# A gated eight-layer network on one core: third attention and third feed-forward on pairs of batches, fourth attention three steps behind, and 128-row bias products

## Chip, core and metric

One core of a Trainium2 chip runs the whole program in one launch. The metric is the time of an execution on the device in microseconds, median of several executions. TensorE's clock has two levels, 1.2 and 2.4 GHz; the profile gives the granted clock as a share of the higher one.

## What is computed

The input x is 8 batches of 128 tokens with 128 features, the context the same shape. Four cross-attentions and four feed-forward layers alternate, each added to x with a gate:

```
x = x + tanh(g_xattn[i]) * attention_i(layernorm(x), ctx, ctx, mask)
x = x + tanh(g_ffn[i])   * ffn_i(layernorm(x))
```

Attention 0 has 16 heads of 64, attentions 1 and 3 have 16 heads of 8 with projections and output bias. Attention 2, which is called the third here, has one head of 128, uses the context itself as keys and values, and then a 128x128 output product with bias: `softmax(Q K^T / sqrt(D)) V @ W.T + b`. Feed-forward 0 and 3 are quantized products 128 to 512 to 128; 1 is a mixture of 8 experts, two per token; 2, called the third, is `layernorm(gelu(x @ fc.T)) @ proj.T` with ternary weights.

## The kernel before

All data stay in on-chip memory. Every engine runs an instruction stream of its own, in order; semaphores join them. The layers are numbered `A0, F0, A1, ROUTE, MOE, A2, F2, A3, F3`. A plan says which layers run in a step: layer L with offset `at` works in steps `at` to `at + 8 + LAG[L]`, one new batch per step. Inside a step each layer has four slots per engine; an entry `(lag, function)` runs the function for the batch that entered `lag` steps ago. `walk` takes the slots of all layers of a step in turn, one instruction from each, and so writes the order of each engine's stream. The third stretch of the program, after the experts, is

```
LAG = [3, 2, 3, 1, 2, 3, 2, 3, 2]
... + steps_of({A2: 0, F2: 4, A3: 8, F3: 12}))
```

So the third attention (A2) starts in step 0, the third feed-forward (F2) in step 4, the fourth attention (A3) in step 8, the fourth feed-forward (F3) in step 12, and there are 22 steps. A2's chain (normalize `xn`, transpose, `scores2` with the mask product, `shift2` for the maximum, `exps2`, `probsT2`, `pv2`, `norm2`, `ot`, `y`, `resid`) is spread over lags 0 to 3. F2's (`up`, `gelu2`, `hid2_stats`, `rs_hid`, `hid2_ln`, `ht`, `y_ffn`) over lags 0 to 2. A3's scores are four products of 4 heads (`scores`, groups 0 to 3) against `kz`, the keys spread over heads by GpSimd (`mask_keys`, two products of 128x1024 per batch). `inverse_root` on GpSimd gives 1/sqrt of each variance. GpSimd fetches the experts' rows for batch b two steps ahead (`fetch`). Biases come in through a product of a 1-row tile of ones with a 1-row tile (`row["bo_n"]`, `crow`), placed before the output product.

## Time and profile before

| | us |
|---|---|
| median of 3 executions | 603.82 (601.82 to 604.89) |
| the profiled execution, its own time | 603.31 |
| its span from first to last instruction | 601.5 |
| mean granted TensorE clock | 0.854 |

The span is read as three stretches: the first plan (attention 0 to routing) up to about 335 us, the experts up to about 380 us, then the third stretch, which the change rewrites. Line numbers in the rows are those of the kernel before: L838 is the bias product and L840 the output product of an attention, L868 up, L879 the transposes of the hidden layer, L887 and L890 bias and down product, L759 scores of A1 and A3, L850 scores of A2, L473 kz.

### The profile page before, as it was taken

What the parts mean: (1) busy time and instruction counts of PE and PEld (TensorE: products, weight loads), DVE (VectorE), ACT (ScalarE), POOL (GpSimd) and SP (SyncE); (2) the same over time, 40 slices, a digit from 0 to 9 for tenths busy, and PEclk for the clock granted to TensorE, in tenths of its full rate; (3) what the DMA queues carried; (4) which work ended last, traced back from release to release, by engine and by line L of the source; (5) the groups of instructions that cost most, each with busy time, mean ns of one, the idle gap of its engine ahead of it and who ended that gap; (6) DMA issues with size and microseconds to landing.
All of it is one profiled execution on the core that took longest, in us unless ns stands there. A gap on an engine that the chain in (4) does not pass through costs nothing.

```text
span 601.5 us, 8470 instructions
## 1 busy us (share of the span) xinstructions
PE 487.6 (81%) x2862; PEld 381.3 (63%) x2862; DVE 373.2 (62%) x1000; ACT 267.8 (45%) x525; POOL 187.7 (31%) x274
## 2 busy tenths in 40 slices
PE   5789899999976897788896499358879988888843
PEld 3577888778865675566685399335646766656721
DVE  1177787788778667667764211355468786886573
ACT  3355455455442444233341243035556665565452
POOL 6080000000213321344514200374244345453141
PEclk9999999999988978788895599855779998996755
DMA  8930000000000200000000231110000000000000
GB/s 357 391 132 2 1 0 2 2 0 1 2 1 0 107 2 0 1 9 6 13 10 18 92 103 60 36 35 19 1 0 1 2 1 0 2 0 1 2 0 35
DMA packets 7131, 21.74 MB, mean 36 GB/s; under 512 B 1217, under 2 KB 3505, under 8 KB 6706
## 3 DMA queue, kind: packets, MB, share of 16 engines
q1 hardware_dynamic: 6065, 19.11, 8.8%
q0 software_dynamic: 1024, 2.10, 1.2%
q8 instruction: 24, 0.39, 0.3%
q14 instruction: 18, 0.14, 0.1%
HBM read 14.33 MB, written 6.88 MB: 35 GB/s over the span
## 4 chain that ended last, share of the span: by engine, by line
PE 56%; DVE 19%; issue 9%; ACT 7%; POOL 5%; DMA 3%; SPq 0%; DVEq 0%; POOLq 0%; ACTq 0%
PE bank L759 7%; PE bank L784 6%; PE bank L767 5%; PE bank L754 4%; PE bank L801 4%; PE bank L924 3%; PE bank L780 3%; DVE xn L1095 3%; PE bank L915 3%; POOL rstd L442 3%; PE bank L796 3%; DVE prob L1126 2%; PE bank L747 2%; PE bank L890 2%; PE bank L735 2%
## 5 line engine op out<-in xcount | busy, mean ns | idle before, releaser
L440 POOL TENSOR_SCALAR rstd<-mv 128x1 f32<-128x1 f32 x64 | 13.2, 206 | 292.7 <-DVE mv L1080 290.2
L1120 DVE TENSOR_REDUCE mx<-bank 128x4 f32<-128x512 f32 x96 | 66.0, 688 | 61.2 <-PE bank L759 43.3
L527 ACT ACTIVATE prob<-prob 128x512 f32<-128x512 f32 x96 | 60.1, 626 | 60.9 <-DVE prob L1126 60.5
L519 ACT ACTIVATE probT<-bank 128x512 f32<-128x512 f32 (+1 forms) x104 | 59.0, 568 | 50.2 <-PE bank L767 48.8
L759 PE MATMUL bank<-kz,qT 128*128 128x512 f32 x128 | 76.6, 685 | 0.0
L767 PEld LDWEIGHTS bank<-pack,prob 128*128 128x128 f32 x384 | 52.1, 154 | 38.1 <-issue 27.8
L784 PEld LDWEIGHTS bank<-va,probT 128*128 128x128 f32 x512 | 71.8, 216 | 0.8 <-ACT probT L519 0.7
L784 PE MATMUL bank<-va,probT 128*128 128x9 f32 x512 | 69.9, 264 | 0.4 <-ACT probT L519 0.4
L1126 DVE TENSOR_TENSOR prob<-bank,mx 128x512 f32<-128x512 f32 x96 | 65.2, 679 | 2.5 <-PE bank L767 1.5
L767 PE MATMUL bank<-pack,prob 128*128 128x128 f32 x384 | 64.1, 294 | 1.3 <-ACT hid L617 1.3
L473 POOL TENSOR_TENSOR kz<-kT,pack 128x1024 f32<-128x1024 f32 x32 | 60.4, 1897 | 0.0
L1095 DVE TENSOR_SCALAR xn<-pack,mv,rstd 128x128 f32<-128x128 f32 x56 | 42.5, 773 | 17.7 <-POOL rstd L442 17.4
L519 ACT ACTIVATE xnT<-bank 128x128 f32<-128x128 f32 x48 | 13.2, 276 | 79.3 <-PE bank L735 75.3
L442 POOL TENSOR_TENSOR rstd<-rstd,minus_half 128x1 f32<-128x1 f32 x72 | 40.3, 560 | 6.0
L754 PE MATMUL bank<-kz,qT 128*128 128x256 f32 x128 | 33.3, 383 | 0.0
L780 PE MATMUL bank<-va,probT 128*128 128x65 f32 x256 | 32.8, 272 | 0.0
L780 PEld LDWEIGHTS bank<-va,probT 128*128 128x128 f32 x256 | 31.9, 196 | 0.0
L489 POOL DMA_INDIRECT moe_rows<-yrows_d,row_of x16 | 15.8, 985 | 51.7 <-DMA yrows_d<-o_n 47.9
L1103 DVE SCALAR_TENSOR_TENSOR pack<-bank,tanh_g,pack 128x128 f32<-128x128 f32 x40 | 13.8, 346 | 26.6 <-PE bank L840 14.6
L735 PE MATMUL bank<-pack,xn 128*128 128x128 f32 x40 | 14.3, 358 | 19.5 <-DVE xn L1095 14.9
L879 PE MATMUL bank<-pack,hid 128*128 128x128 f32 x96 | 19.8, 344 | 11.3 <-DVE hs L1244 5.1
L759 PEld LDWEIGHTS bank<-kz,qT 128*128 128x128 f32 x128 | 25.5, 218 | 4.8 <-issue 2.5
(212 smaller groups left out, 956.2 us busy)
## 6 DMA issues: line engine op xcount, KB each, us to landing
yrows_d<-moe_rows SPq DMA_DIRECT2D x2, 1510.0 KB, 19.8
pack<-pack_d SPq DMA_DIRECT2D x1, 2112.0 KB, 14.7
expert<-experts_d SPq DMA_DIRECT2D x4, 514.0 KB, 8.8
pack<-experts_d SPq DMA_DIRECT2D x4, 514.0 KB, 4.3
pack<-pack_d SPq DMA_DIRECT2D x1, 2048.0 KB, 9.6
xrows_d<-moe_rows SPq DMA_DIRECT2D x1, 1080.0 KB, 18.3
moe_rows<-xrows_d SPq DMA_DIRECT2D x8, 135.0 KB, 3.1
yrows_d<-o_n SPq DMA_DIRECT2D x8, 135.0 KB, 1.8
```

The source lines that it names most:

```text
L442: pool.tensor_tensor(out, out, minus_half, ALU.pow).then_inc(ev.sem, 1)
L473: pool.tensor_tensor(kz[:, it.k, 1024 * half:1024 * half + 1024].rearrange("p (h t) -> p h t", h=heads), kT[:, bass.ds(it.b, 1), :].to_bro ...
L519: act.activation(dst, src, ACT.Identity if kw else ACT.Copy, **kw).then_inc(E[layer][name].sem, 1)
L527: act.activation(prob[:, g % 2, :], prob[:, g % 2, :], ACT.Exp, scale=float(DK0 if layer == A0 else DK) ** -0.5).then_inc(E[layer]["probs" ...
L754: mm_ = pe.matmul(out[:, 256 * c:256 * c + 256], qT[:, it.k, P * t:P * t + P], kz[:, it.k, 256 * t:256 * t + 256], start=False, stop=(c == 1))
L759: mm_ = pe.matmul(out[:, :], qT[:, it.k, 0:P], kz[:, it.k, 512 * g:512 * g + 512], start=neg is None, stop=True)
L767: mm_ = pe.transpose(bank[T_BANK[g % 2]][:, P * j:P * j + P], prob[:, g % 2, P * j:P * j + P], ident)
L780: mm_ = pe.matmul(bank[O_BANK[g % 2]][:, VW0 * j:VW0 * j + VW0], probT[:, g % 2, P * j:P * j + P], va0[:, it.k, h, :], start=True, stop=True)
L784: mm_ = pe.matmul(bank[O_BANK[it.k]][:, VW * h:VW * h + VW], probT[:, g % 2, P * j:P * j + P], va[:, bass.ds(it.b, 1), h, :], start=True, ...
L1095: yield from do(dve.tensor_scalar(out, xs(it), mv[z][:, k, 0:1], rstd[z][:, k, 0:1], ALU.subtract, ALU.mult), hold=layer in (F0, F3))
L1120: yield from do(dve.tensor_reduce(m, src, AX.X, ALU.max))
L1126: yield from do(dve.tensor_tensor(prob[:, g % 2, :].rearrange("p (h t) -> p h t", h=GH), src, m.rearrange("p (h a) -> p h a", a=1).to_broa ...
```

## The change

- A2 and F2 work on two batches at a time (`PAIRS = 4` repetitions). Tiles get twice the width; each product, transpose, exp, gelu and normalization is still issued per batch, while evacuations of 128 columns, the maximum, the reciprocal, the division, the residual and the square root take both batches in one instruction.
- A2's lag is 1: scores, maximum, exp and transpose of a pair happen in the step in which it is normalized; PV to residual in the next.
- The offsets are A2 0, F2 1, A3 3, F3 7, which makes 17 steps.
- The softmax denominator comes from a column of ones behind the context, by PV, instead of from the exp's accumulator.
- All output biases of attentions 1 to 3 and `crow` are 128-row tiles with one row filled, multiplied by the 128x128 ones. `bv_3` stays one row.
- In routing, VectorE does the statistics ahead of the choice of experts.

```
-LAG = [3, 2, 3, 1, 2, 3, 2, 3, 2]
+PAIRS = B // 2
+REPS = [B, B, B, B, NE, PAIRS, PAIRS, B, B]
+LAG = [3, 2, 3, 1, 2, 1, 2, 3, 2]
...
-        + steps_of({A2: 0, F2: 4, A3: 8, F3: 12}))
+        + steps_of({A2: 0, F2: 1, A3: 3, F3: 7}))
...
 (GpSimd)
-                A2: [[(0, rs, A2)], [(0, fetch_ahead)], [], []],
-                F2: [[(0, rs, F2)], [], [(1, rs_hid)], []],
+                A2: [[(0, rs_2), (0, fetch_ahead)], [], [], []],
+                F2: [[], [], [(1, rs_hid)], [(0, rs_f)]],
 (ScalarE)
-                A2: [[(1, xt_sb, A2), (2, exps2)], [], [(3, ot_sb, A2), (2, probsT_sb2)], []],
-                F2: [[], [(1, gelu2), (2, hT_sb2)], [], [(0, xt_sb, F2)]],
+                A2: [[], [(1, ot_sb2), (0, xt_sb2)], [None, (0, exps2)], [(0, probsT_sb2)]],
+                F2: [[(2, hT_sbf, 1), (1, xt_sbf)], [(1, gelu_f, 0)], [(1, gelu_f, 1)], [(1, hT_sbf, 0)]],
 (TensorE)
-                pe.matmul(out, ones[0:1, :], row[f"bo_{n}"], start=True, stop=False)
+                pe.matmul(out, ones, col[f"bo_{n}"], start=True, stop=False)
...
+            def yf(it):
+                claim(it, F2, "y")
+                out = bank[R_BANK[1]][:, 0:W2]
+                pe.matmul(out.rearrange("p (a n) -> p a n", a=2), ones, both(crow[:, :]), start=True, stop=False)
+                for i in range(2):
+                    wait(pe, F2, "ht_sb", it, 1 + i)
+                    for t in range(FT):
+                        mm_ = pe.matmul(out[:, P * i:P * i + P], hT_f[it.k][:, F * i + P * t:F * i + P * t + P],
+                                        projw[:, P * t:P * t + P], start=False, stop=(i == 1 and t == FT - 1))
...
-                A2: [[(1, xt, A2)], [(3, ot, A2), (2, probsT2)], [(1, scores2)], [(2, pv2), (3, y, A2)]],
-                F2: [[(1, up, F2, "up", tern["fcT"][:, :], xnT[1])], [(2, ht, F2)], [None, None, (2, y_ffn, F2, projw)], [(0, xt, F2)]],
+                A2: [[(1, pv2)], [(1, ot2), (0, xt2)], [(1, y2), (0, scores2)], [(0, probsT2)]],
+                F2: [[(2, htf, 1), (2, yf), (1, xtf)], [(1, upf, 0)], [(1, upf, 1)], [(1, htf, 0)]],
 (VectorE)
-                A2: [[[(3, norm2), (0, sum_stats)]], [(0, ln, A2)], [], [(1, shift2), (3, resid, A2)]],
-                F2: [[(0, ln_stats, F2)], [(0, ln, F2)], [[(1, hid2_stats), (2, resid, F2)]], [(1, hid2_ln)]],
+                A2: [[[(1, norm2), (0, sum_stats)]], [(0, pair_ln, A2, xn_2, mv_2, rstd_2)], [(1, pair_resid, A2), (0, shift2)], []],
+                F2: [[(2, pair_resid, F2), (1, pair_ln, F2, xn_f, mv_f, rstd_f)], [(1, hid_stats, 0)], [(1, hid_stats, 1)],
+                     [(1, hid_ln), (0, stats_of_f)]],
...
-                ROUTE: [[(1, choose), (0, ln_stats, ROUTE)], [(0, ln, ROUTE), (1, row_numbers)], [], []],
+                ROUTE: [[(0, ln_stats, ROUTE), (1, choose)], [(0, ln, ROUTE), (1, row_numbers)], [], []],
```

**Where instructions stand.** First place: VectorE where a step begins and A2 and F2 run (no fourth attention scores yet). Before, step 6 or so; pack0 is x, bank7 the output bank, rden the denominators, L1323 the expert sum:

```order
L1103 SCALAR_TENSOR_TENSOR pack0<-bank7,tanh_g,pack0 128x128
L1177 RECIPROCAL rden<-rden 128x1
L1079 BN_STATS stats1<-pack0 128x6
L1323 SCALAR_TENSOR_TENSOR pack0<-moe_rows,w_tok,pack0 128x128
L1080 BN_AGGR mv1<-stats1 128x2
```

Now, step 3 of the new plan (L1299 with bank7 is the residual of F2's pair, L1448 the expert sum, oT here holds the divided output):

```order
L1279 RECIPROCAL rden_2<-bank4 128x2
L1299 SCALAR_TENSOR_TENSOR pack0<-bank7,tanh_g,pack0 128x256
L1182 BN_STATS stats0<-pack0 128x6
L1448 SCALAR_TENSOR_TENSOR pack0<-moe_rows,w_tok,pack0 128x128
L1292 TENSOR_SCALAR qT<-pack0,mv_f,rstd_f 128x128
L1183 BN_AGGR mv0<-stats0 128x2
L1280 TENSOR_TENSOR oT<-bank4,rden_2 128x256
```

The feed-forward's residual, which stood in the third slot, is now the second instruction of the step, ahead of the sums, the normalization and the division.

Second place: ScalarE in a step with A3 and F2. Before, step 11 (hid is gelu's result, in the rows below va0 is, prob the exponentials of a head group):

```order
L527 ACTIVATE prob<-prob 128x512
L519 ACTIVATE probT<-bank2 128x512
L617 ACT_TABLE_LOAD
L617 ACTIVATE hid<-bank3 128x512
L527 ACT_TABLE_LOAD
L527 ACTIVATE prob<-prob 128x512
```

One gelu stands there between two exponentials. Now, the same engine at the same place in new step 5:

```order
L613 ACT_TABLE_LOAD
L613 ACTIVATE va0<-bank2 128x512
L556 ACT_TABLE_LOAD
L556 ACTIVATE prob<-prob 128x512
L548 ACTIVATE probT<-bank3 128x512
L613 ACT_TABLE_LOAD
L613 ACTIVATE va0<-bank3 128x512
L556 ACT_TABLE_LOAD
L556 ACTIVATE prob<-prob 128x512
```

One gelu between two exps has become two gelus, each in front of an exp, with four table loads.

Third place: TensorE in the same kind of step, at its scores of group 3 and the beginning of the next step. Before (L879 are the hidden transposes, in slot 1, behind the scores of group 1), step 10:

```order
L832 MATMUL bank6<-pack0,o_n 128x128
L879 MATMUL bank2<-pack0,hid 128x128 x4
L759 MATMUL bank1<-kz,qT 128x512
L767 MATMUL bank3<-pack0,prob 128x128 x4
L784 MATMUL bank4<-va_3,probT 128x9 x4
```

Now, new step 5 into 6 (L955 are the transposes of each half, L802 the scores, L961 and L965 bias and down product):

```order
L778 MATMUL bank6<-pack0,xn0 128x128
L955 MATMUL bank0<-pack0,va0 128x128 x4
L802 MATMUL bank1<-kz,qT 128x512
L810 MATMUL bank3<-pack0,prob 128x128 x4
L869 MATMUL bank7<-xnT0,pack2 128x128
L827 MATMUL bank5<-va_3,probT 128x9 x4
L955 MATMUL bank1<-pack0,va0 128x128 x4
L802 MATMUL bank0<-kz,qT 128x512
L961 MATMUL bank7<-crow,pack0 128x256
```

The transposes of the first half stand right in front of the scores of group 3, those of the second in front of the next step's first scores, and the down product right behind these.

## Rows read from the trace of the kernel before

**Rows 1.** The page: busy time and granted clock in 40 slices.
```profile
PE 487.6 (81%) x2862; PEld 381.3 (63%) x2862; DVE 373.2 (62%) x1000; ACT 267.8 (45%) x525; POOL 187.7 (31%) x274
PEclk9999999999988978788895599855779998996755
```

**Rows 2.** Windows of the third stretch: busy us (instructions) per engine, then clock.
```profile
386.90:445.20 58.30, 41.08 (x144) 27.63 (x145) 31.22 (x109) 24.99 (x58) 29.97 (x51) 0.59 0.06 16
445.20:458.60 13.40, 11.36 (x54) 6.63 (x52) 9.63 (x19) 8.24 (x17) 5.96 (x8) 0.95 0.00 1
458.60:472.30 13.70, 13.23 (x82) 9.59 (x81) 10.84 (x23) 9.10 (x16) 5.96 (x8) 1.00 0.00 1
472.30:486.40 14.10, 13.22 (x83) 9.75 (x81) 10.74 (x22) 9.21 (x16) 5.95 (x8) 1.00 0.01 2
486.40:499.50 13.10, 12.05 (x80) 9.19 (x79) 11.17 (x29) 9.02 (x16) 6.01 (x10) 1.00 0.00 1
499.50:516.00 16.50, 14.30 (x82) 10.61 (x81) 10.39 (x30) 8.84 (x19) 8.61 (x12) 0.90 0.00 0
516.00:544.60 28.60, 22.67 (x151) 16.95 (x150) 25.40 (x72) 17.36 (x36) 15.85 (x22) 1.00 0.01 1
544.60:598.40 53.80, 36.66 (x162) 25.39 (x161) 31.40 (x111) 25.98 (x49) 16.12 (x31) 0.57 0.00 1
```

**Rows 3.** Timeline, TensorE products at granted clock 0.50.
```profile
414.26 1.91 PE L868 MATMUL bank<-t_fcT,xnT 128*128 128x512 f32 x2
417.34 1.06 PE L879 MATMUL bank<-pack,hid 128*128 128x128 f32 x4
418.41 0.31 PE L849 MATMUL bank<-neg,identb 128*128 128x128 bf16 x1
418.52 0.74 PE L850 MATMUL bank<-pack,xnT 128*128 128x128 f32 x2
420.85 2.08 PE L890 MATMUL bank<-projw,hid 128*128 128x128 f32 x8
423.50 0.79 PE L838 MATMUL bank<-rows_sb,pack 1*128 1x128 f32 x2
424.22 0.80 PE L840 MATMUL bank<-pack,oT 128*128 128x128 f32 x2
```

**Rows 4.** Timeline, down and up products at full clock.
```profile
466.14 1.16 PE L890 MATMUL bank<-projw,hid 128*128 128x128 f32 x8
432.62 1.02 PE L868 MATMUL bank<-t_fcT,xnT 128*128 128x512 f32 x2
```

**Rows 5.** Timeline, ScalarE: exp, table load, gelu, evacuations.
```profile
417.22 0.37 ACT L562 ACTIVATE prob<-bank,mx 128x128 f32<-128x128 f32 x1
417.70 1.28 ACT L617 ACT_TABLE_LOAD   x1
418.99 0.60 ACT L617 ACTIVATE hid<-bank 128x512 f32<-128x512 f32 x1
419.49 0.59 ACT L519 ACTIVATE hid<-bank 128x512 f32<-128x512 f32 x1
419.96 0.28 ACT L519 ACTIVATE oT<-bank 128x128 f32<-128x128 f32 x1
```

**Rows 6.** Timeline, VectorE: first and last of eight small instructions.
```profile
416.02 0.15 DVE L1177 RECIPROCAL rden<-rden 128x1 f32<-128x1 f32 x1
417.71 0.18 DVE L1080 BATCH_NORM_AGGREGATE mv<-stats 128x2 f32<-128x6 f32 x1
```

**Rows 7.** Timeline: 512-wide normalization alone, and beside GpSimd's kz; square root.
```profile
423.49 0.19 POOL L440 TENSOR_SCALAR rstd<-mv_h 128x1 f32<-128x1 f32 x1 [3.78 <-DVE mv_h L1252]
423.77 0.55 POOL L442 TENSOR_TENSOR rstd<-rstd,minus_half 128x1 f32<-128x1 f32 x1
424.35 0.55 DVE L1258 TENSOR_SCALAR hid<-hid,mv_h,rstd 128x512 f32<-128x512 f32 x1 [0.77 <-POOL rstd L442]
469.26 1.90 POOL L473 TENSOR_TENSOR kz<-kT,pack 128x1024 f32<-128x1024 f32 x1
469.40 2.04 DVE L1258 TENSOR_SCALAR hid<-hid,mv_h,rstd 128x512 f32<-128x512 f32 x1
```

**Rows 8.** Fetch of batch 1's second half, and landing times of L489.
```profile
386.83 0.94 POOL L489 DMA_INDIRECT moe_rows<-yrows_d,row_of  x1 [0.30 <-issue]
DMA to landing us min/median/max: 2.4/2.5/2.9
```

**Rows 9.** Windows before and in two stretches of low clock, second attention.
```profile
260.70:264.10 3.40, 2.60 (x15) 1.58 (x14) 3.02 (x3) 0.48 (x1) 3.40 (x3) 1.00 0.00 0
264.10:274.30 10.20, 9.05 (x34) 7.18 (x35) 4.97 (x11) 3.47 (x8) 3.02 (x3) 0.58 0.04 13
...
291.30:294.80 3.50, 2.87 (x19) 1.85 (x17) 3.09 (x3) 0.60 (x1) 3.42 (x4) 1.00 0.00 0
294.80:301.60 6.80, 5.49 (x20) 4.16 (x21) 3.63 (x8) 2.19 (x5) 3.03 (x3) 0.61 0.06 19
```

More of the change, by code:

```diff
@@ L87, in steps_of @@
 def steps_of(offsets):
-    last = max(at + B + LAG[n] for n, at in offsets.items())
-    return [("steps", [(n, t - at) for n, at in offsets.items() if 0 <= t - at < B + LAG[n]]) for t in range(last)]
+    last = max(at + REPS[n] + LAG[n] for n, at in offsets.items())
+    return [("steps", [(n, t - at) for n, at in offsets.items() if 0 <= t - at < REPS[n] + LAG[n]]) for t in range(last)]
 def turns(*parts):
@@ L495, in first_fetches @@
                     pool.wait_ge(y_stored[k], 16 * (NE // 2))
-                fetch(0)
-                fetch(1)
+                for b in range(3):
+                    fetch(b)
             def fetch_ahead(it):
-                if it.rep + 2 < B:
-                    fetch(it.rep + 2)
+                for b in (2 * it.b + 3, 2 * it.b + 4):
+                    if b < B:
+                        fetch(b)
             stages = {
@@ L847, in scores2 @@
                     pe.wait_ge(pool_const, 7 + B)
[L848 to L851 removed]
+                for i in range(2):
+                    out = bank[S_BANK[it.k]][:, P * i:P * i + P]
+                    pe.matmul(out, identb[:, :], neg2[:, 2 * it.b + i, :], start=True, stop=False)
+                    mm_ = pe.matmul(out, xnT_2[:, it.k, P * i:P * i + P], ctxT[:, 2 * it.b + i, :], start=False, stop=True)
+                mm_.then_inc(E[A2]["scores"].sem, 1)
             def probsT2(it):
@@ L855, in probsT2 @@
                 claim(it, A2, "t")
-                pe.transpose(bank[O_BANK[1 - it.k]][:, 0:P], prob[:, it.k, 0:P], ident).then_inc(E[A2]["probsT"].sem, 1)
+                for i in range(2):
+                    mm_ = pe.transpose(bank[T_BANK[it.k]][:, P * i:P * i + P], prob_2[:, it.k, P * i:P * i + P], ident)
+                mm_.then_inc(E[A2]["probsT"].sem, 1)
             def pv2(it):
@@ new lines, in pv2, with ot2, both, y2 @@
+                mm_.then_inc(E[A2]["pv"].sem, 1)
+            def ot2(it):
+                wait(pe, A2, "norm", it)
+                claim(it, A2, "ot")
+                for i in range(2):
+                    mm_ = pe.transpose(bank[R_BANK[0]][:, P * i:P * i + P], o_2[:, it.k, P * i:P * i + P], ident)
+                mm_.then_inc(E[A2]["ot"].sem, 1)
+            def both(tile):
+                return tile.rearrange("p (a n) -> p a n", a=1).to_broadcast([P, 2, P])
+            def y2(it):
+                claim(it, A2, "y")
+                out = bank[R_BANK[1]][:, 0:W2]
+                pe.matmul(out.rearrange("p (a n) -> p a n", a=2), ones, both(col["bo_2"]), start=True, stop=False)
+                wait(pe, A2, "ot_sb", it)
+                for i in range(2):
+                    mm_ = pe.matmul(out[:, P * i:P * i + P], oT_2[:, it.k, P * i:P * i + P], col["woT_2"],
+                                    start=False, stop=(i == 1))
+                mm_.then_inc(E[A2]["y"].sem, 1)
@@ new lines, in xtf, with upf, htf @@
+            def xtf(it):
+                xt_pair(it, F2, xn_f)
+            def upf(it, i):
+                wait(pe, F2, "xt_sb", it)
+                claim(it, F2, f"up{i}")
+                pe.matmul(bank[T_BANK[i]][:, :], xnT_f[:, it.k, P * i:P * i + P], tern["fcT"][:, :], start=True, stop=True
+                          ).then_inc(E[F2]["up"].sem, 1)
+            def htf(it, i):
+                wait(pe, F2, "hid", it, 5 + i)
+                claim(it, F2, f"ht{i}")
+                for t in range(FT):
+                    mm_ = pe.transpose(bank[S_BANK[i]][:, P * t:P * t + P], hid_f[it.k][:, F * i + P * t:F * i + P * t + P], ident)
+                mm_.then_inc(E[F2]["ht"].sem, 1)
@@ new lines, in norm2, with pair_stats @@
+                r = rden_2[:, it.k, :].rearrange("p (i a) -> p i a", a=1)
+                yield from do(dve.reciprocal(r, src[:, :, P:P + 1]))
+                yield from do(dve.tensor_tensor(o_2[:, it.k, :].rearrange("p (i n) -> p i n", i=2), src[:, :, 0:P],
+                                                r.to_broadcast([P, 2, P]), ALU.mult), hold=False)
+            def pair_stats(do, it, st, mean_var):
+                for i in range(2):
+                    yield from do(dve.bn_stats(st[:, it.k, i, :], x_sb[:, 2 * it.b + i, :]))
+                    yield from do(dve.bn_aggr(mean_var[:, it.k, i, :], st[:, it.k, i, :]), hold=False)
@@ new lines, in pair_ln, with pair_resid @@
+            def pair_ln(it, layer, out, mean_var, r):
+                wait(dve, layer, "rs", it)
+                do = chain(layer, "ln", it, 4)
+                for i in range(2):
+                    yield from do(dve.tensor_scalar(out[:, it.k, P * i:P * i + P], x_sb[:, 2 * it.b + i, :], mean_var[:, it.k, i, 0:1],
+                                                    r[:, it.k, i:i + 1], ALU.subtract, ALU.mult), hold=False)
+            def pair_resid(it, layer):
+                wait(dve, layer, "y", it)
+                x2 = x_sb[:, 2 * it.b:2 * it.b + 2, :]
+                n = {A2: 2, F2: 6}[layer]
+                dve.scalar_tensor_tensor(x2, bank[R_BANK[1]][:, 0:W2].rearrange("p (i n) -> p i n", i=2), tanh_g[:, n:n + 1], x2,
+                                         ALU.mult, ALU.add).then_inc(E[layer]["resid"].sem, 1)
@@ L1184, in quant0, with stats_of_f @@
+            def stats_of_f(it):
+                wait(dve, A2, "resid", it)
+                yield from pair_stats(chain(F2, "ln", it), it, stats_f, mv_f)
             def quant0(it):
```

207 lines of the change are left out of this document (125 added, 82 removed).

## Prediction

> **What bounds the kernel now.** I read the page first: TensorE is the busiest engine, and its clock is granted only in parts of the span [rows 1]. The change touches the third stretch of the program (the plan that begins after the experts), so I then took the windows of that stretch, cut where a step's first scores of the fourth attention start [rows 2]. I call the steps of the old plan old 0 to 21, those of the new plan new 0 to 16. The reader is to see three things. From 386.9 us (first fetched rows arrive) to 445.2 us, old steps 0 to 8 run third attention and feed-forward alone: 58.3 us at a mean clock of 0.59, TensorE 70% busy. From 445.2 us on, each step holds one batch of the fourth attention, and takes 13.1 to 16.5 us, nearly the same whether a third feed-forward batch runs beside it (13.7, 14.1 us) or a fourth one (28.6 us for two steps). There TensorE is busy 92 to 97% as long as a third feed-forward batch is beside it, and no wait is long. The last 53.8 us are one more such step and the drain; both plans have them alike.
>
> **Part 1: steps.** The new plan has 17 steps instead of 22, but the steps from the first scores of the fourth attention on are the same in number: old 9 to 21 become new 4 to 16, always one batch per step. So five fewer steps means only that old 0 to 8 become new 0 to 3, and that in old 9 to 11, which become new 4 to 6, pairs take the place of single batches. I add up new 0 to 6 and compare them with 386.9 to 486.4 us (99.5 us).
>
> **Durations.** At 1.2 GHz (granted clock 0.50) a transpose holds TensorE for 0.21 us (four 1.06 us together), up 1.91, four products of the down projection 2.08, scores 0.31 + 0.74, bias 0.79, output product 0.80 [rows 3]; at 2.4 GHz down takes 1.16 and up 1.02 [rows 4]. ScalarE: table load 1.28, exp 0.37, gelu 0.60, a 512-wide evacuation 0.59, a 128-wide one 0.28 [rows 5]; 256-wide forms don't occur for it, their bounds are 0.28 and 0.59, I take 0.38 by straight line. VectorE: eight small instructions from a reciprocal to the second aggregate take 1.87 us, 0.23 each [rows 6]; the 512-wide normalization takes 0.55 us alone and 2.04 us beside a kz product of GpSimd (1.90 us, and both end together) [rows 7]. A square root on GpSimd is 0.19 + 0.55 [rows 7], with the hops 0.9 us from aggregate to use.
>
> **New 0 (11.9 us).** A pair needs the rows of batch 1 too. Its second fetch is issued at 386.83 us and a fetch lands 2.5 us after its issue [rows 8], so 389.4. Two sums and the statistics 1.3, root 0.9, two normalizations 0.65, two transposes 0.65, evacuation 0.45, scores of two batches 1.4 (two times 0.31 + 0.74, overlapped), maximum and scale 0.7, table load and two exps 2.0, transposes 0.7, evacuation 0.4: 398.8 us.
>
> **New 1 (12.1 us).** Here the lag of the attention, 3 before, 1 now, shows. PV of the pair 1.1; then VectorE's reciprocal, and behind it in its queue the sums and statistics of the next pair, ten instructions, 3.0; root 0.9; normalization 0.7; transposes 0.7; output product of the pair with its bias 1.9, in front of the scores in TensorE's order; scores 1.3; maximum 0.7; exps 0.7; transposes and evacuation 1.1. They stand in one line; before, they were spread over four steps of different batches.
>
> **New 2 (18.3 us).** As new 1, plus: the second normalization of the attention now stands behind the statistics of the first gelu (up 1.9, load 1.28, gelu 0.6 after it), +2.8; up of the second batch stands between output product and scores, +1.9; exp needs a table load again, +1.3. Rounded: 429.2 us.
>
> **New 3 (24.7 us).** The down projection of pair 0 stands first on TensorE: PV 1.1, transposes 1.1, evacuation 0.6, the 256-wide bias and 16 products 4.4 (at 1.2 GHz; 2.3 at 2.4 GHz), and VectorE's residual waits for it with 13 instructions queued behind it (3.65, since some depend on each other; first order excerpt). Root, transpose, up, gelu with its load, output, second up, scores, exp with its load as in new 2 (14); then the 512-wide normalization beside kz, 2.0. The clock probably rises within this step: 27 us with all of it at 1.2 GHz, 22.5 with all at 2.4; I take the middle. First scores of the fourth attention: 453.9 us, against 445.2.
>
> **New 4 and 5 (19.5 us each; second and third order excerpt).** Per step, from the first scores at 0 and at full clock: down projection to 3.2; residual 3.7, which VectorE does before it may reduce the scores; feed-forward normalization 5.2; transposes and evacuation 6.0; up 7.1; load and gelu 9.0; load and exp of head group 0 10.9; load and gelu of the second batch 13.4, since ScalarE's order alternates them; its statistics and root 15.2; kz starts then on GpSimd, by its order, so the normalization ends with it at 17.2; transposes 17.8; only behind them TensorE computes the scores of group 3, 18.7; the second half and its transposes start the next step at about 19.5 to 20.5. Sum of TensorE's own work in such a step: old 13.2 of 13.7 us with one feed-forward batch, whose products are some 3 us, gives about 16: the chain is longer than the work.
>
> **New 6 (15 us), 7 to 10 (56 us).** New 6 has only the down projection of the last pair, at its head: 14.1 + 1. New 7 to 10 are old 12 to 15, which took 13.1 + 16.5 + 28.6 = 58.2, of which 2.2 fall away with the last single feed-forward batches.
>
> **Part 2: table loads.** ScalarE's order has 13 loads in this stretch instead of 17: 4 times 1.28 = 5.1 us less [rows 5]. They are inside the steps counted above; of the four in new 4, and in new 5, three stand on the chain. The row shows an activation starting 0.01 us after its load. The Trainium skill ("ScalarE: Activation LUTs", section "What ACT_TABLE_LOAD costs") puts a switch at about 2.66 us with the drain; by that these six loads would add 8 us more. The rows show no such gap.
>
> **Part 3: full bias products.** A 1-row bias pair and the 128-row output pair take the same 0.79 and 0.80 us [rows 3], so nothing in duration. What they may do to the clock is a rival below. **Part 4: order in routing.** Statistics before the choice of experts: the root on GpSimd stands behind the attention's root and the scatters anyway; 1 us at most in the drain. The wider packs load ahead of their use, and the cleared crow is hidden behind the first load: 0. If those loads were not hidden, 0.5 us.
>
> **Sum.** New 0 to 6: 11.9 + 12.1 + 18.3 + 24.7 + 39 + 15 = 121. 386.9 + 121 + 56 + 53.8 - 1 = 616.7 us, where before the last result is ready at 598.4. With the 3.1 us of the store the span is 619.8, against 601.5. The profiled execution took 603.31 us, 1.8 above its span, so 621.6 for its like, and the median of the runs shown is 0.5 above that execution. Forecast: 621 us.
>
> **Rivals.** A (faster, 20%): the steps last as long as the work of their busiest engine and the in-step order is hidden. Place: new 1 to 6. For it speaks that old steps with the fourth attention are 92 to 97% full. Price: TensorE's work at 1.2 GHz is 6.3, 11.6, 17.2 us in new 1, 2, 3, then 15.6 twice and 14.1; with new 0 the seven steps are 92, the time 593. It decides below 99.5 + 2.2 + 1 = 102.7 us for these seven steps. Against it: VectorE and ScalarE run in order, and in new 3 thirteen instructions stand behind a wait for the down projection. B (slower, but little, 15%): the clock is granted from new 2 on, since products come denser; up, output, scores and down halve: 9 us less, 612. C (7%): full bias products hold the clock in the second attention: the window before a fall (291.3 to 294.8 us) holds a bias product, and the 6.8 us behind it ran at 0.61 [rows 9]; so it is from 260.7 us on (10.2 us at 0.58). Half of these 17 us is 8.5; with B that gives 604, no change. Against it: the falls at other places have no bias product ahead. D (58%): my forecast; below it, the slack of new 3; above it, one more fall of the clock, as in old 13 (16.5 us instead of 13.1), and new 4 at 1.2 GHz, 5 us more.
>
> **Numbers.** 621; D's own range is 613 to 631. A, 20%, is left out below; 602 to 631 holds the rest. About 0.5% (3 us) is what a measurement of this kernel tells from no change: faster 0.20, same 0.07, slower 0.73.
>
> **What would show it.** In the changed profile: first scores of the fourth attention after 450 us (right) or before 440 (A); steps new 4 and 5 of 18 us or more, with VectorE waiting for the down product before its 256-wide residual and TensorE for the 512-wide normalization; later steps of 13 to 14.5 us; 13 table loads. The prediction is wrong if new 1 to 3 take under 14 us each, or if the clock is whole between 200 and 320 us.

## The result and the profile after

The changed kernel takes **617.36 us** (617.16 to 618.76), the kernel before 602.82 us beside it; the ratio is 1.0228, 95% interval 1.0189 to 1.0268. The forecast was 621 us, between 602 and 631. Side and size are right. That the sum comes so near is in part luck: a part that I had put too low and parts that I had put too high cancel, and the 617 us themselves are a loss and a gain of which I had priced only the loss.

First the page of the changed kernel, TensorE's busy time and its granted clock in 40 slices (compare [rows 1]):

```profile
span 617.0 us, 8268 instructions
PE 476.5 (77%) x2832; PEld 379.2 (61%) x2846; DVE 368.1 (60%) x977; ACT 260.6 (42%) x497; POOL 180.3 (29%) x250
PEclk9899999999987987777885799556877969989955
```

Next the windows of the third stretch of the changed kernel, cut where a step's first scores of the fourth attention start, as in [rows 2]: busy us (instructions) per engine, then clock.

```profile
388.70:454.90 66.20, 34.28 (x129) 24.30 (x130) 28.39 (x90) 18.50 (x35) 25.50 (x36) 0.63 0.06 14
454.90:478.80 23.90, 15.37 (x70) 10.14 (x69) 11.82 (x25) 11.57 (x17) 5.36 (x6) 0.82 0.00 1
478.80:502.50 23.70, 17.77 (x93) 13.54 (x92) 11.03 (x23) 12.68 (x19) 6.23 (x8) 0.83 0.00 0
502.50:515.40 12.90, 12.90 (x85) 10.15 (x83) 8.11 (x15) 5.90 (x12) 4.47 (x4) 0.92 0.00 1
515.40:527.20 11.80, 10.12 (x65) 7.63 (x66) 9.54 (x26) 5.66 (x12) 5.95 (x8) 1.00 0.01 1
568.00:614.00 46.00, 28.07 (x158) 20.54 (x161) 31.26 (x112) 25.67 (x49) 16.13 (x31) 0.66 0.00 1
```

The light steps end at 454.9 us (forecast 453.9). New 4 and 5 take 23.9 and 23.7 us with TensorE busy 15.4 and 17.8: no engine is full, unlike in [rows 2]. Everything behind is shorter than before.

For the comparison of many kernels I use five marks in each: the first fetch of the experts' rows, the maximum of head group 0 in the first, fourth and last batch of the fourth attention, and the store. In the timeline of the kernel before, then of the changed one:

```profile
383.03 0.99 POOL L489 DMA_INDIRECT moe_rows<-yrows_d,row_of  x1 [47.85 <-DMA yrows_d<-o_n]
446.92 0.69 DVE L1120 TENSOR_REDUCE mx<-bank 128x4 f32<-128x512 f32 x1 [2.33 <-PE bank L759]
487.46 0.69 DVE L1120 TENSOR_REDUCE mx<-bank 128x4 f32<-128x512 f32 x1 [0.29 <-PE bank L759]
546.62 0.69 DVE L1120 TENSOR_REDUCE mx<-bank 128x4 f32<-128x512 f32 x1
598.47 0.36 SPq L406 DMA_DIRECT2D out_d<-pack  x1
```

```profile
385.46 0.98 POOL L517 DMA_INDIRECT moe_rows<-yrows_d,row_of  x1 [48.81 <-DMA yrows_d<-o_n]
459.55 0.68 DVE L1223 TENSOR_REDUCE mx<-bank 128x4 f32<-128x512 f32 x1
516.50 0.69 DVE L1223 TENSOR_REDUCE mx<-bank 128x4 f32<-128x512 f32 x1 [0.91 <-PE bank L802]
570.07 0.69 DVE L1223 TENSOR_REDUCE mx<-bank 128x4 f32<-128x512 f32 x1
613.92 0.36 SPq L425 DMA_DIRECT2D out_d<-pack  x1
```

The differences of these rows, for all kernels of the study (medians in us; stretches from the one profiled execution; clock: mean of that execution):

| kernel | median | clock | fetch to 1st | 1st to 4th | 4th to last | last to store |
|---|---|---|---|---|---|---|
| before | 602.8 | 0.854 | 63.9 | 40.5 | 59.2 | 51.9 |
| route_order_before | 603.8 | 0.841 | 63.9 | 43.1 | 62.1 | 46.4 |
| full_bias_before | 596.4 | 0.875 | 61.2 | 39.0 | 57.1 | 44.2 |
| no_gelu_tables_full_bias_before | 585.2 | 0.872 | 57.3 | 37.6 | 58.3 | 43.7 |
| more_full_products_before | 597.3 | 0.892 | 63.6 | 43.0 | 62.0 | 48.3 |
| changed | 617.4 | 0.845 | 74.1 | 57.0 | 53.6 | 43.8 |
| bias_96_rows_after | 618.1 | 0.845 | 74.2 | 57.0 | 53.6 | 43.8 |
| bias_64_rows_after | 628.4 | 0.829 | 78.3 | 59.7 | 54.7 | 45.7 |
| row_bias_after | 629.7 | 0.824 | 78.4 | 63.1 | 54.6 | 45.7 |
| full_bias_pairs_only_after | 620.4 | 0.845 | 74.0 | 55.7 | 53.6 | 45.8 |
| fourth_attention_at_7 | 620.0 | 0.839 | 104.7 | 27.8 | 54.8 | 43.6 |
| no_gelu_tables_after | 618.9 | 0.842 | 74.0 | 56.8 | 53.6 | 43.6 |
| transposes_behind_scores | 615.5 | 0.843 | 74.0 | 56.8 | 56.4 | 43.8 |
| keys_at_step_end | 622.1 | 0.842 | 73.7 | 56.3 | 58.4 | 44.2 |

Executions of the kernel before differ more than those of the others: 594.8 to 611.2 us in 19 of them, at a mean clock of 0.867 and 0.834. The ratios below go by fast executions alone (within 1.5% of the fastest of their kernel), so a ratio can say less than two medians do. The profiled execution is not always a typical one: that of full_bias_before took 588.74 us, the fastest of its 12, where the median is 596.4, so its stretches flatter it. The kernel before, measured again beside three groups of experiments, had medians of 604.0, 604.0 and 603.6 us instead of 602.8, so about 1 us of any difference from the changed kernel's 617.4 can be the occasion. The first fetch itself lies anywhere between 378 and 387 us in these runs; the 2.4 us by which it came later in the changed kernel are of that size.

### The profile page after: what moved, and what is told of

It is laid out like the page before. It is cut to its first block, busy times and chain, and to the rows that moved or that the text cites. A ratio compares the mean times of both kernels' runs of the same rounds, so it can differ in the third digit from the quotient of the medians.

```text
span 617.0 us, 8268 instructions
## 1 busy us (share of the span) xinstructions
PE 476.5 (77%) x2832; PEld 379.2 (61%) x2846; DVE 368.1 (60%) x977; ACT 260.6 (42%) x497; POOL 180.3 (29%) x250
## 4 chain that ended last, share of the span: by engine, by line
PE 52%; DVE 23%; issue 9%; ACT 7%; POOL 4%; DMA 3%; another core or an unknown queue 0%; SPq 0%; DVEq 0%; ACTq 0%; POOLq 0%
PE bank L802 5%; PE bank L827 5%; PE bank L844 4%; PE bank L810 4%; PE bank L797 4%; PE bank L1025 3%; PE bank L823 3%; PE bank L1016 3%; DVE prob L1227 3%; DVE xn L1198 3%; PE bank L839 3%; POOL rstd L462 2%; DVE mx L1223 2%; PE bank L790 2%; DMA pack<-pack_d 2%
## 5 line engine op out<-in xcount | busy, mean ns | idle before, releaser
L459 POOL TENSOR_SCALAR rstd<-mv 128x1 f32<-128x1 f32 (+1 forms) x52 | 10.8, 208 | 307.4 <-DVE mv L1183 286.6
L556 ACT ACTIVATE prob<-prob 128x512 f32<-128x512 f32 x96 | 60.1, 626 | 61.2 <-DVE prob L1227 60.7
L802 PE MATMUL bank<-kz,qT 128*128 128x512 f32 x128 | 76.7, 685 | 0.8 <-DVE prob L1227 0.7
L548 ACT ACTIVATE probT<-bank 128x512 f32<-128x512 f32 x96 | 56.7, 591 | 47.3 <-PE bank L810 47.1
L810 PE MATMUL bank<-pack,prob 128*128 128x128 f32 x384 | 62.8, 290 | 1.7 <-ACT sg L648 0.4
L1198 DVE TENSOR_SCALAR xn<-pack,mv,rstd 128x128 f32<-128x128 f32 x40 | 36.2, 924 | 6.0 <-POOL rstd L462 6.0
L462 POOL TENSOR_TENSOR rstd<-rstd,minus_half 128x1 f32<-128x1 f32 (+1 forms) x52 | 29.9, 576 | 4.3
L802 PEld LDWEIGHTS bank<-kz,qT 128*128 128x128 f32 x128 | 25.5, 219 | 5.3 <-issue 1.9
L548 ACT ACTIVATE qT<-bank 128x512 f32<-128x512 f32 (+2 forms) x28 | 13.3, 475 | 33.5 <-PE bank L890 17.9
L790 PE MATMUL bank<-neg,identb 128*128 128x512 bf16 x64 | 26.1, 408 | 1.3 <-ACT va L682 0.7
L797 PEld LDWEIGHTS bank<-kz,qT 128*128 128x128 f32 x128 | 24.8, 194 | 2.9
L548 ACT ACTIVATE kz<-bank 64x512 f32<-64x512 f32 x32 | 18.9, 591 | 14.8 <-PE bank L844 14.4
## 6 DMA issues: line engine op xcount, KB each, us to landing
pack<-pack_d SPq DMA_DIRECT2D x1, 2112.0 KB, 15.4
```

The costliest lines, as they stand in the source:

```text
L462: pool.tensor_tensor(out, out, half, ALU.pow).then_inc(ev.sem, 1)
L548: act.activation(dst, src, ACT.Identity if kw else ACT.Copy, **kw).then_inc(E[layer][name].sem, 1)
L556: act.activation(prob[:, g % 2, :], prob[:, g % 2, :], ACT.Exp, scale=float(DK0 if layer == A0 else DK) ** -0.5).then_inc(E[layer]["probs" ...
L797: mm_ = pe.matmul(out[:, 256 * c:256 * c + 256], qT[:, it.k, P * t:P * t + P], kz[:, it.k, 256 * t:256 * t + 256], start=False, stop=(c == 1))
L802: mm_ = pe.matmul(out[:, :], qT[:, it.k, 0:P], kz[:, it.k, 512 * g:512 * g + 512], start=neg is None, stop=True)
L810: mm_ = pe.transpose(bank[T_BANK[g % 2]][:, P * j:P * j + P], prob[:, g % 2, P * j:P * j + P], ident)
```

## Experiments

**1. Bias products of one row in the changed kernel.**

```
-                pe.matmul(out, ones, col[f"bo_{n}"], start=True, stop=False)
+                pe.matmul(out, ones[0:1, :], col[f"bo_{n}"][0:1, :], start=True, stop=False)
```
(and the same for `bo_2` and `crow`.)

> The changed kernel with its bias products 1 row high again (attentions 1 to 3 and third feed-forward), nothing else. Theory (bias products neither cost nor keep the clock): the changed kernel's time, 617.4 us, within 2 us; first fetch of the experts' rows again near 385.5 us, last fourth-attention stretch (from the first scores of the last batch to the end) again about 46 us. Rival (full products hold the clock in the second attention and at the end): 621 to 626 us, with that last stretch back near 54 us. Second rival (full products cost the 2.4 us by which the fetches come later than in the kernel before): 615 us and fetches at 383.

Measured: 629.65 us (628.14 to 630.63), ratio 1.0486 [1.0353, 1.0619]: 12 us slower than the changed kernel, with no overlap. My theory fell. The rival has the direction, but the time is 4 us above its range and the place is another one: the last stretch is 45.7 us in the table, 1.9 more than in the changed kernel, and the rest lies in the steps before. TensorE's windows from 10 us before the clock rises show where: first the changed kernel, then the one with rows.

```profile
416.10:426.40 10.30, 8.04 (x22) 4.44 (x21) 4.24 (x14) 3.63 (x6) 2.88 (x4) 0.52 0.05 13
426.40:436.60 10.20, 5.64 (x32) 5.23 (x32) 4.35 (x18) 3.48 (x6) 1.79 (x4) 0.83 0.01 2
```

```profile
414.50:424.80 10.30, 7.73 (x18) 3.59 (x18) 4.33 (x15) 3.03 (x5) 2.89 (x4) 0.50 0.04 13
424.80:435.00 10.20, 7.48 (x31) 6.12 (x30) 3.20 (x11) 4.09 (x7) 1.79 (x4) 0.50 0.01 2
435.00:445.20 10.20, 5.03 (x17) 2.79 (x15) 5.99 (x19) 2.65 (x4) 3.50 (x5) 0.50 0.00 0
```

Nearly the same products stand in the first two windows of both (22 and 32 against 18 and 31). With full products the clock rises to 2.4 GHz at about 426 us, with 1-row products it stays at 1.2 GHz until about 451, although TensorE is busy 7.5 of 10.2 us from 424.8 us on. Added up from the first fetch on, the half-clock time is 109 us with full products and 147 with rows.

**2. Full bias products in the kernel before.** The edit of experiment 1 the other way round, with `bo_1`, `bo_2`, `bo_3` and `crow` as 128-row tiles.

> The kernel before with all those bias products 128 rows high, nothing else. Theory: 603 us within 2, fetches at 383.0 us, last stretch near 54 us. Rival (the clock is held by them): 595 to 598 us, fewer half-clock stretches between 165 and 335 us, last stretch near 46 us. Second rival (they cost the 2.4 us): 605 us, fetches at 385.4.

Measured: 596.39 us (588.74 to 598.90, 12 executions), the kernel before beside it 603.96 (594.75 to 611.23, 19 executions); ratio 0.9960 [0.9917, 1.0002]. The medians differ by 7.5 us, but the ratio only by 0.4% (2.4 us), and its interval does not exclude zero: no difference in time is shown here. The profile, which is of the fastest execution, has the earlier rise of the clock (the half-clock stretch in which the third stretch begins is 23.9 us long instead of 44.4) and 44.2 us in the last stretch instead of 51.9. Fewer half-clock stretches between 165 and 335 us, which the rival named, it does not have: 62.4 us of them, 62.5 in the kernel before. The direction is that of experiment 1, its size here is not settled.

**3. 64 rows, and 4. 96 rows.**

```
-                pe.matmul(out, ones, col[f"bo_{n}"], start=True, stop=False)
+                pe.matmul(out, ones[0:64, :], col[f"bo_{n}"][0:64, :], start=True, stop=False)
```

> The changed kernel with its bias products 64 rows high (not 128, not 1). The products of 1 and of 128 rows last equally long, 629.7 and 617.4 us for the whole. If the clock goes by how much of the array works, this lies between them, 621 to 626 us; if by whether the product is more than a sliver, 617 to 618; if only whole products count, 629 to 630.

> The changed kernel with its bias products 96 rows high. 1 row gave 629.7 us, 64 rows 628.4, 128 rows 617.4. If the clock goes by the share of the array in steps: near 617 us like the full ones. If it goes gradually with the rows: 620 to 624. If only a product over all rows counts: 628 to 630 us.

Measured: 64 rows 628.44 us (627.11 to 630.38), nearly as with 1 row. 96 rows 618.05 us (three of four between 615.18 and 619.37, one 625.56), ratio 1.0210 [1.0166, 1.0254], as with 128; its four stretches agree with the changed kernel's within 0.1 us. So in time nearly all of the effect comes between 64 and 96 rows. In the clock of the one profiled execution 64 rows lie in between: half-clock time from the first fetch on is 147 us with 1 row, 133 with 64, 109 with 96 and with 128, and the long half-clock stretch at the beginning takes 64.9, 51.2, 41.0 and 41.0 us. That stretch with 64 rows, and the changed kernel's (windows):

```profile
389.70:440.70 51.00, 28.05 (x90) 18.34 (x90) 17.37 (x61) 11.56 (x22) 18.92 (x26) 0.50 0.08 20
385.50:426.50 41.00, 18.62 (x58) 11.89 (x58) 14.19 (x49) 8.07 (x16) 19.20 (x24) 0.51 0.10 26
```

In all profiles here that stretch goes with the bias products of the third attention and third feed-forward: 37.5 to 41.0 us in the seven kernels on pairs with 96 or 128 rows there, 17.1 to 23.9 in the three single-batch kernels with 128 rows, and 44.4 and 51.2 in the two with 1 row. The bias product of the pairs (L935, groups by form: min/median/max ns) in the kernels with 1, 64, 96 rows and in the changed one:

```profile
L935 PE MATMUL bank<-pack x8: 372/629/792, 406.3 to 469.2; 1*128 1x256 f32 x8
```

```profile
L935 PE MATMUL bank<-pack x8: 373/631/792, 409.5 to 472.2; 64*128 64x256 f32 x8
```

```profile
L935 PE MATMUL bank<-pack x8: 377/634/636, 408.1 to 465.1; 96*128 96x256 f32 x8
```

```profile
L935 PE MATMUL bank<-pack x8: 377/632/635, 407.8 to 464.5; 128*128 128x256 f32 x8
```

Four equal durations (medians 629, 631, 634, 632 ns), two different kernel times. The Trainium skill ("TensorE: Matmul & The Clock Gate", section "Why this matters for your kernels") says that a product with 32 rows lasts as long as one with 128; these rows agree for 1, 64 and 96. That sentence prices the product and not what it does to the clock, which is what I had done too.

**5. Full products only in the pairs.** The first diff for attentions 1 and 3 alone.

> The changed kernel with 128-row bias products in the third attention and third feed-forward, and 1-row ones in the second and fourth attention. From the first fetch to the first maximum of the fourth attention it took 74.1 us with full products everywhere and 78.4 with 1 row, the three following steps 57.0 and 63.2, the last stretch from the last batch's first maximum 43.8 and 45.7. Theory (the pairs' products are what counts up to the fourth maximum, the fourth attention's in the last stretch): 74 and 57 us, 45.7 in the last stretch, 619 to 621 us. Rival (the fourth attention's own products hold the clock beside the pairs): 74, 63, and 625 us.

Measured: 620.41 us (615.25 to 627.64), ratio 1.0243 [1.0176, 1.0309]; 74.0 and 55.7 us up to the fourth maximum, as with full products everywhere, and 45.8 in the last stretch, as with rows everywhere. The theory holds in its stretches and by the median, though the four executions scatter over 12 us: of the 12 us the pairs' products bring some 10, up to the fourth maximum (78.4 + 63.1 against 74.1 + 57.0), the fourth attention's own bring 2 in the last stretch.

**6. The order in routing.** `ln_stats` ahead of `choose` in the kernel before.

> The kernel before with the routing's statistics ahead of the choice of experts on VectorE, nothing else. If the order of routing is what makes the fetches come 2.4 us later in the changed kernel: fetches at about 385.4 us and 605 us. If it costs nothing, as the prediction said (1 us at most): fetches at 383.0 to 384.0 us and 603 to 604 us.

Measured: 603.81 us (596.94 to 607.23), ratio 1.0051 [0.9992, 1.0109]: no difference clear of noise, though the interval reaches 1.1% slower. The fetch began at 387 us in the profiled execution, within the scatter named above.

**7 and 8. No gelu tables,** in the changed kernel and in the kernel before with full bias products.

```
-                ... ACT.Gelu).then_inc(E[F2]["gelu"].sem, 1)
+                ... ACT.Copy).then_inc(E[F2]["gelu"].sem, 1)
```

> The changed kernel with the third feed-forward's gelu replaced by a plain copy of the same size (the layer's function is left out), so that ScalarE loads its tables once in the third stretch instead of 13 times. Theory (six loads of 1.28 us stand on the chain of new 4 and 5, and one or two each in new 2, 3 and 6): 8 to 12 us less, 606 to 609 us, with new 4 and 5 at 19 to 21 us instead of 23.9 and 23.7. Rival (the chain over VectorE and TensorE is as long, the loads lie beside it): 615 to 617 us. Rival (what sets these steps is the clock): the steps shrink by more than the loads' time, 600 us or less.

> The kernel before with the full bias products (596.4 us) and the same gelu replaced by a copy (the function is left out): 1 load instead of 17 in the third stretch. Theory (before, the loads lay beside TensorE's work, since one gelu stood between two exponentials): 594 to 596 us. If the loads cost the kernel before as much as the changed one, it falls by 8 to 12 us, to 585 to 588, and the loads explain nothing of the 21 us between the two structures.

Measured: the changed kernel 618.94 us (615.31 to 620.39) without 12 of its 13 loads, so no gain; the other one 585.22 us (583.98 to 592.58) against 596.39, which was measured on another chip. Both came out opposite to my theory: where the loads were to cost they cost nothing, and where they were to lie beside the work the time falls by 11 us. So the loads explain nothing of the 21 us between the two structures with full bias products; without loads these are 34 us apart. In the changed kernel the loads did stand in the chain: from the first maximum to the root of new 4 it takes 8.8 us instead of 10.9. The timeline of new 4 without loads shows where the 2.1 us went:

```profile
465.22 0.19 POOL L459 TENSOR_SCALAR rstd_h<-mv_h 128x2 f32<-128x2 f32 x1 [3.58 <-DVE mv_h L1374]
466.22 2.10 DVE L1381 TENSOR_SCALAR va<-va,mv_h,rstd_h 128x512 f32<-128x512 f32 x1 [0.46 <-POOL rstd_h L462]
468.38 1.12 PE L955 MATMUL bank<-pack,va 128*128 128x128 f32 x4 [3.88 <-DVE va L1381]
474.73 1.91 PE L802 MATMUL bank<-kz,qT 128*128 128x512 f32 x2
```

TensorE still idles 3.9 us for the normalization, the clock falls as before, and the next step's first scores now run at 1.2 GHz (1.91 us, where the changed kernel has 1.02 at the same place). From the first scores to the end of the normalization the step takes 16.8 us instead of 18.6, from there to the next first scores 6.4 instead of 5.3: most of the time that was saved ahead of the fall was lost behind it. By the Trainium skill ("ScalarE: Activation LUTs", section "What ACT_TABLE_LOAD costs"), 2.66 us a switch, 12 loads would have been an estimated 32 us of ScalarE; the measurement decides: a load takes 1.28 us, and nothing of it reaches the end here. In the kernel before, the stretches to the first and to the fourth maximum shrink by 3.9 and 1.4 us; the profiled executions themselves took 588.74 and 586.20 us, so they can't explain the 11 us between the medians, and why the loads cost there stays open.

**9. The fourth attention four steps later** (`A3: 7, F3: 11`).

> The changed kernel with the fourth attention entering in step 7 and the fourth feed-forward in step 11, so 21 steps and no pair beside the fourth attention. Theory (pairs beside the fourth attention make three steps of 23.9, 23.7 and 12.9 us, which single batches take in 13 each; pairs alone cost 12 to 20 us a step): three more light steps of 16 to 20 us and three fourth-attention steps of 11 to 12: about 60 us take the place of 60, 614 to 624 us. Rival (overlap hides the pairs almost wholly): 640 us and more. Rival (the overlap is what costs): 605 us or less.

Measured: 619.97 us (618.59 to 622.13), within the theory's range. From the fetch to the fourth maximum it takes 132.5 us, in the changed kernel 131.1: pairs and three batches of the fourth attention side by side take as long as one after the other. Without pairs beside it, a batch takes 9.0 and 9.2 us. Of the four steps by which the fourth attention follows closer, nothing arrives but 1.4 us.

**10. Transposes behind the scores.** On TensorE a turn later, in F2's last slot:

```
-                ... [(1, upf, 1)], [(1, htf, 0)]],
+                ... [(1, upf, 1)], [None, (1, htf, 0)]],
```

> The changed kernel with the transposes of the first half of the hidden pair placed one turn later on TensorE, behind the fourth attention's scores of group 3 and its transposes of group 1, nothing else. Theory (in new 4 and 5 the scores of group 3 wait for the 512-wide normalization that stands in front of them, 5.75 us idle ahead of them in new 4): the reduction of group 3 comes some 3 us earlier, but the down product one place later; 2 to 3 us less per step, 612 to 614 us. Rival (the chain over gelu, statistics and root is as long without it, since the transposes only swap places with what waits for them): 616 to 618 us. Rival (the clock sets these steps): within 1 us too, with clock falls at the same places.

Measured: 615.52 us (614.24 to 617.41), ratio 1.0252 [1.0124, 1.0380]; the fetch came 3.9 us earlier, and from there on it is not faster: 74.0, 56.8, 56.4 and 43.8 us, where the changed kernel has 74.1, 57.0, 53.6 and 43.8. The edit did what it was to do, as the timeline of new 4 shows (first scores at 450.73):

```profile
463.72 1.02 PE L802 MATMUL bank<-kz,qT 128*128 128x512 f32 x2
467.46 2.10 DVE L1381 TENSOR_SCALAR va<-va,mv_h,rstd_h 128x512 f32<-128x512 f32 x1 [0.45 <-POOL rstd_h L462]
469.49 0.68 DVE L1223 TENSOR_REDUCE mx<-bank 128x4 f32<-128x512 f32 x1
469.62 1.12 PE L955 MATMUL bank<-pack,va 128*128 128x128 f32 x4 [4.88 <-DVE va L1381]
474.26 1.91 PE L802 MATMUL bank<-kz,qT 128*128 128x512 f32 x2
```

The scores of group 3 are done ahead of the transposes, and their maximum comes 13.9 us after the step's first one instead of 16.9, the 3 us of the theory. But TensorE then has nothing to do until the normalization ends (4.88 us idle), and runs at 1.2 GHz from there to the next step's first scores without a gap. The step is 23.5 us long instead of 23.9. So the step goes by the chain over gelu, statistics and root and by the clock behind it; the two rivals can't be told apart here. The median lies between the theory's 612 to 614 us and the rivals' 616 to 618.

**11. Keys at the end of the step.**

```
-                A3: [[(0, rs, A3)], [(0, mask_keys, A3, kT_3, 0)], [(0, mask_keys, A3, kT_3, 1)], []],
+                A3: [[(0, rs, A3)], [(0, mask_keys, A3, kT_3, 0)], [], [(0, mask_keys, A3, kT_3, 1)]],
```

> The changed kernel with the second kz product of GpSimd in the last slot of the step instead of the third, so that it no longer starts together with the 512-wide normalization that waits for GpSimd's root. Theory (in new 4 and 5 TensorE idles 5.75 and some 4 us for this chain): the normalization takes 0.55 us instead of 2.1 three times, and with less idle the clock falls less: from the fourth attention's first to fourth maximum 50 to 54 us instead of 57.0, whole 612 to 615 us. Rival (the slow normalization only moves to another neighbour, or the kz comes late for the scores of the next step): 616 to 619 us.

Measured: 622.09 us (619.87 to 623.89), ratio 1.0322 [1.0285, 1.0358], so 5 us slower than the changed kernel and above the rival's range too. The timeline of new 4 has the normalization alone, and TensorE still waiting:

```profile
468.01 0.55 DVE L1381 TENSOR_SCALAR va<-va,mv_h,rstd_h 128x512 f32<-128x512 f32 x1 [0.45 <-POOL rstd_h L462]
468.61 1.12 PE L955 MATMUL bank<-pack,va 128*128 128x128 f32 x4 [4.18 <-DVE va L1381]
```

In new 5 the later kz of GpSimd again meets it (2.11 us), and from the fourth to the last maximum it takes 58.4 us instead of 53.6; why is not shown. New 4 is 23.8 us long as before: 17.4 us to the end of the normalization instead of 18.6, and 6.4 behind it instead of 5.3. The rival's mechanism holds, its time does not.

**12. More full products in the kernel before.** Three products of zeros behind each full bias product:

```
+                for _ in range(3):
+                    pe.matmul(out, ones, zero[:, :], start=False, stop=False)
```

> The kernel before with full bias products and three more 128-row products of zeros behind each of them, in the second to fourth attention and in the third feed-forward, where the bias product and these stand ahead of the wait for the hidden evacuation. Its sums stay the same. Theory (products over all rows in TensorE's idle time keep the clock): half-clock time from the first fetch on 50 us or less instead of 75, 586 to 592 us by the median, against 596.4. Rival (they only take TensorE's time, 0.3 to 0.6 us each in its busy steps): 600 to 606 us.

Measured: 597.32 us (596.59 to 599.68), ratio 0.9897 [0.9865, 0.9929]: about 1% faster than the kernel before, by an interval that excludes no change, though within the 594.8 to 611.2 us that the kernel before covered beside experiments 1 and 2. It is no faster than full bias products alone, and both ranges of time missed. So did the theory's place: from the first fetch on the half-clock time is 78 us, not 50 or less, and 75 with full bias products alone. What it gained lies ahead of the fetch, 51 us of half-clock time instead of 72; from the fetch to the store it takes 216.9 us, the kernel before 215.4. The page has a mean clock of 0.892, the highest here, and 178 more records of TensorE products than [rows 1] (each of the 96 added products makes two, and some are missing from the trace). The first steps with the fourth attention take 14.0 to 14.9 us between maxima, where full bias products alone give 12.3 to 14.3.

```profile
span 597.8 us, 8835 instructions
PE 483.3 (81%) x3040; PEld 391.6 (66%) x3054; DVE 374.5 (63%) x1002; ACT 267.6 (45%) x525; POOL 187.2 (31%) x274
```

## Why the prediction was right, and where not

**New 0 to 3: right.** The steps were to end at 453.9 us and ended at 454.9, with the fetch 2.4 us late. By the start of PV (L918 at 401.51, 413.60 and 430.24 us), new 1 and 2 took 12.1 and 16.6 us, forecast 12.1 and 18.3, and new 3 took 24.7 up to the first scores of the fourth attention, as forecast. The clock rose at about 426 us, at the end of new 2 and so a little before "probably rises within this step" (new 3); it then fell again for 3.4, 3.4 and 6.8 us before 457. New 3 ran at half clock for 11 of its 24.7 us, so the middle between 22.5 and 27, which I took for want of better, came out by luck. The measured 617.4 us lie between my 621 and the 612 of rival B, in which the clock is granted from new 2 on.

**New 4 and 5: the mechanism right, the size wrong.** The step is "Per step, from the first scores at 0 and at full clock", 19.5 us. The chain of the changed kernel, in new 4 (timeline; first scores at 454.94):

```profile
459.15 0.48 DVE L1299 SCALAR_TENSOR_TENSOR pack<-bank,tanh_g,pack 128x256 f32<-128x256 f32 x1 [4.64 <-PE bank L965]
459.55 0.68 DVE L1223 TENSOR_REDUCE mx<-bank 128x4 f32<-128x512 f32 x1
464.47 0.60 ACT L613 ACTIVATE va<-bank 128x512 f32<-128x512 f32 x1
468.32 0.60 ACT L613 ACTIVATE va<-bank 128x512 f32<-128x512 f32 x1
470.41 0.19 POOL L459 TENSOR_SCALAR rstd_h<-mv_h 128x2 f32<-128x2 f32 x1 [5.68 <-DVE mv_h L1374]
471.42 2.10 DVE L1381 TENSOR_SCALAR va<-va,mv_h,rstd_h 128x512 f32<-128x512 f32 x1 [0.45 <-POOL rstd_h L462]
473.57 1.11 PE L955 MATMUL bank<-pack,va 128*128 128x128 f32 x4 [5.75 <-DVE va L1381]
474.48 1.92 PE L802 MATMUL bank<-kz,qT 128*128 128x512 f32 x2
477.04 0.54 DVE L1381 TENSOR_SCALAR va<-va,mv_h,rstd_h 128x512 f32<-128x512 f32 x1
478.79 1.02 PE L802 MATMUL bank<-kz,qT 128*128 128x512 f32 x2
```

Each link is there: VectorE waits 4.64 us for the down product ahead of the residual, and only then takes the maximum of scores that started at 454.94; two gelus with their loads; root; normalization beside kz (2.10 us, forecast 2.04); TensorE idle 5.75 us for it; scores of group 3 behind the transposes. Until the normalization ends the forecast was 17.2 us, measured 18.6, of which 0.9 is the first scores at 1.2 GHz; in new 5, whose first scores run at full clock (478.79), it ends after 17.3. What I missed is behind: during the idle time the clock falls (6.8 us at half in new 4, 10.2 in new 5), and the next step's first scores start 5.3 us after the normalization ends in new 4 and 6.4 in new 5, where I had put 2.3. TensorE has no gap there, so it is its own work that sets this part (experiment 10, with the group's maximum out of the way, has 4.7). By the starts of the same products at full clock elsewhere in the changed kernel (transposes 0.47 and 0.47, scores 0.86, transposes of exponentials 0.44, L869 0.22, PV of a head group 0.82), an estimate of this work is 3.3 us. So 1 us of what I missed is the products that stand between in the order excerpt and that I left out, and 2 us in new 4 and 3 in new 5 are the clock. "At full clock" was the failed assumption, for steps in which I had myself found TensorE waiting. New 4 to 6 are 60.5 us instead of 54. That experiments 7 and 11 shorten the chain of new 4 by 1.8 and 1.2 us and the step by no more than 0.7 fits this: what comes earlier is lost to the clock behind it.

**The last part.** "The last 53.8 us are one more such step and the drain; both plans have them alike" is wrong: 46.0 us. New 7 to 10 took 52.6 us, forecast 56. These 7.8 and 3.4 us more than make up for the 6.5 of new 4 to 6 and the 1.0 of the start, and that is luck. The sum also takes off 1 us without a reason, and its last step (621.6 and 0.5 more) gives 622.1, not 621; both are small beside its range. "Busy 92 to 97%" leaves out the first such step, where [rows 2] has 11.36 of 13.40 us, 85%. Experiment 5 gives 2 us of it to the fourth attention's bias products. In the kernel with rows everywhere it took 100.3 us from the fourth maximum to the store, before 111.0, in the changed kernel 97.4. Some of the 10.7 us is the last single batches, which I had put at 2.2 us; the rest moves with where the falls of the clock lie (route_order_before, the same third stretch as before, has 108.5), and I can't split it further.

**Part 3 failed.** "Nothing in duration" is right and was the wrong question; "what they may do to the clock" was rival C, at 7%. Full products are worth 12 us in the changed kernel, four times what the measurement can tell. I had looked for the effect in the second attention, where there is none: between 165 and 335 us the half-clock time is 62.5 us before and 62.5 in the changed kernel, and 61.0 with rows. It lies in the light steps and behind idle gaps. Without full products everything else in the change costs 26 us (629.7 against 604.0 by the medians; by the ratio of 1.0486, 29), and my sum, which took no clock from the biases, would have been 9 us short. So the 617 us are two parts: the rest of the change, +26, and the bias products, -12; my +18 stands between them. Taken the other way round, with full bias products in both, the structures are 21 us apart (617.4 against 596.4). That these 26 us are the pairs and the shorter lag is read from the timelines: of the rest of the change, the closer plan was tested (experiment 9: 1.4 us the other way) and the order in routing (experiment 6), while no run here has pairs with a lag of 3, single batches with a lag of 1, or the denominators from the exp's accumulator again.

**Loads and rival A.** 13 loads, as forecast. That three of four stand "on the chain" of new 4 is too much: without them the root comes 2.1 us earlier, not 3.8, and the end is the same. Rival A fell: TensorE's work is 15.4 of 23.9 us, and the seven steps end at 515.4 instead of before 489.6 us (its bound of 102.7 us behind 386.9). Nothing contradicts Part 4 (experiment 6), which leaves up to 1.1% open.

## What to carry to other kernels

Batching two items per step halves the steps and lengthens the chain in each; here, with engines that run in order and a lag of one step instead of three, the chain and the slow clock behind it were the step, and laying it beside another layer hid 1.4 us (experiment 9). Cost such a step with TensorE's clock as its idle gaps will leave it, not as the full steps of before had it, and with every product that stands in the order. And do not take two products for equal because they last equally long: a bias product over 96 or 128 rows was worth more here than one over 1 or 64, most where TensorE is half idle; further products of zeros brought nothing more (experiment 12).

## What the runs showed of the hardware that was not expected

- Products of 1, 64, 96 and 128 rows take 629 to 634 ns each, yet with 1 or 64 rows the program takes 629.7 and 628.4 us and with 96 or 128 rows 618.1 and 617.4, by the granted clock (mean 0.824 and 0.829 against 0.845). The half-clock time from the first fetch on is 147, 133, 109 and 109 us. The sums are the same, since the added rows of the bias tile are zeros; those of the tile of ones are not, and whether the clock goes by the height or by what the rows hold was not tried, nor were products of 65 to 95 rows.
- TensorE stayed at 1.2 GHz through a stretch in which it was busy 7.5 of 10.2 us (row_bias_after, 424.8 to 435.0 us).
- Executions of one and the same kernel on one core differ by up to 16 us (594.8 to 611.2), along with their mean clock (0.867 to 0.834).
